# Three reorderings in a Mixture-of-Experts and Mamba kernel: copies of B ahead of evacuations on ScalarE, the last two state sums side by side on TensorE, and the fourth B multiply with the SiLU burst one tile on

## The chip, the cores and the metric

The kernel runs on one core of a Trainium2 chip. The metric is the device time of one execution in microseconds (µs). Before the change it is 6058.42 µs, the median of three runs (6050.98 to 6075.53).

## What is computed

Input x is (8, 96, 64, 64) in float32: 8 images of 4096 tokens with 96 channels. Two layers follow one another.

```python
# layer 0: mixture of 4 experts (hidden 192), the two best by router, added to x
logits = tokens @ router_w.T + router_b
gates  = softmax over the two best logits, 0 for the others
for ei in range(4):
    hid = gelu(tokens @ fc1_w[ei].T + fc1_b[ei])
    out = out + gates[..., ei:ei+1] * (hid @ fc2_w[ei].T + fc2_b[ei])
x = x + scale * out

# layer 1: layer norm over channels, a Mamba block forward and on the reversed sequence
xr, z = split(x_norm @ W_in)                  # 192 inner channels each
xr = silu(causal_conv4(xr) + conv_b)
dt = softplus(xr @ W_xproj[:, :6] @ W_dt + b_dt);  B, C = (xr @ W_xproj)[:, 6:]   # 16 states
h  = exp(dt * A) * h + (dt * xr) * B          # the scan over 4096 tokens
y  = sum over states of h * C + xr * D
out = (y * silu(z)) @ W_out
x  = (out_forward + out_reversed) * 0.5 + x
```

## The kernel before, in words

**Tiles.** The state has 192 channels times 16 states, 3072 rows, which make `NT` = 24 tiles of 128 partitions. A sequence is cut into 8 chunks of 512 tokens (`CH`). One *body* treats one chunk in one direction: 24 scans of 128x512. An image has 16 bodies, 8 forward (numbers 0 to 7) and then 8 reverse (8 to 15), and there are 8 images, so 128 bodies. Bodies are written in pairs, an even one (`odd` = 0) and an odd one (`odd` = 1), inside loops over images and pairs (`bodies`). In the text, scan i is the scan of tile i of a body.

**Batches.** Four tiles make a batch, so six batches (`NB`) to a body, numbered s = 0 to 5. The product dt\*x\*B of batches 0 and 1 is made by GpSimd (L1240, 128x2048), that of batches 2 to 5 by VectorE (L1147, 128x2048): these four are "the first to fourth B multiply" here, with `h` = 0 to 3. VectorE reads for them a copy of B that ScalarE puts into the PSUM bank `p_b` (`copy_b`, L927). There is one such bank, so copy h waits for multiply h-1. A multiply also waits for the sum of the batch that used its slot of X before (`summed_before`).

**The round of a tile.** ScalarE computes exp(dt\*A) into one of three PSUM banks (`exp_dA`, L939, two tiles ahead of the scan; exponential i waits for scan i-3). VectorE scans (L1163). When a batch of four is scanned, GpSimd saves the carries (L1248) and multiplies by C (L1250, 128x2048), and TensorE adds the states of that batch into the bank `p_y` (`sum_states`, L708). Sum 1 closes the low channels of y, sum 5 the high channels. After sum 5 the bank is emptied: in a forward body ScalarE evacuates it (`evacuate`, L944) to be stored; in a reverse body VectorE gates it (`gate_y`, L1168) with SiLU(z), and TensorE then makes the output (`finish`, L717 to L719), which ScalarE copies out (`copy_out`, L879). The work on sum 5 of a body lies in the first tiles of the next.

**Around the scans** each pair of bodies also carries the layers of later chunks. In the even body TensorE first sums and multiplies experts into the piece's output (`residual` L650, `expert_out` L656, `expert_bias` L660), ScalarE copies it (`copy_x2`, L868), then comes the layer norm (`ln_mean` L665, `ln_centred` L874 and L875, `ln_var` L669, `ln_rstd` L884 and L887). Each body has three hidden tiles of the experts (L640), with one GELU burst on ScalarE (a table load, three activations and a table load back, L861 and L852), gating rows on TensorE (L647) and three gate instructions on VectorE (L1127). TensorE projects the window for the convolution (L677). Near the end of a body ScalarE has the SiLU burst: a table load and two activations for xr (`silu_x`, L894), in most reverse bodies two for z (`silu_z`, L899), and a load back. TensorE then projects dt, B and C from xr (`project_dt`, L692 and L693), and at the start of the next body ScalarE and VectorE turn that into softplus(dt) (L909, L911, L915, L1135).

**What sets the order.** Nothing is scheduled. Every engine has its own stream written out by hand, in program order, with semaphore waits between engines. On ScalarE and VectorE the steps beside the scans hang on the tile number `i`, in the order of the `if` lines; on TensorE they are a plain list. All DMAs are on SyncE's queue.

The lines that hang on a tile number on ScalarE:

```python
if i == 5 and before == 0:
    evacuate(n - 1, 0, ...)
if i == 5:
    copy_b(n, 0, par)
...
if i == 8:
    if before == 1:
        copy_out(u)
    copy_b(n, 1, par)
```

`before` is 0 where the body before this one ran forward, 1 where it ran in reverse.

## Time and profile before

| what | value |
|---|---|
| median of the runs | 6058.42 µs |
| time of the profiled execution | 6065.3 µs |
| its span, first to last instruction | 6063.5 µs |
| mean granted clock of TensorE | 0.855 of full speed |
| VectorE busy | 5276.6 µs (87%), 4474 instructions |
| GpSimd busy | 5156.9 µs (85%), 2127 |
| TensorE busy | 4967.7 µs (82%), 14273 matmuls |
| ScalarE busy | 4307.0 µs (71%), 6471 |
| DMA | 159 GB/s over the span |

A row of a timeline gives the start from the beginning of the span, the duration, engine, line, operation, what it writes and reads, how many instructions are merged in it, and in brackets how long the engine was idle before it and which instruction released it. The first 190 µs are setup and routing, up to about 380 µs the first image's experts; then the 128 bodies follow until the end. A float32 matmul of this kernel shows as two records.

### The profile page before, as it was taken

The page shows a single profiled execution, that of the slowest core. Times are in us where ns is not written, and L with a number is a line of the kernel's source. Part 1 is how long each engine was busy: PE and PEld are TensorE (multiplying, and loading weights), DVE is VectorE, ACT ScalarE, POOL GpSimd, SP SyncE. Part 2 cuts the span into 40 slices and gives each one's busy share as a digit, 9 for nine tenths or more (in the row PEclk, how much of TensorE's full clock was granted, in tenths as well). Part 3 has the DMA queues.
Part 4 walks back from the last instruction along what each step waited for, and adds up shares of the span by engine and source line. Part 5 has one row for each costly group of instructions (what it writes and reads, how often), then busy time and mean ns, then how long its engine had stood idle before and what let it go on. Part 6 is the DMA issues. An engine that isn't in the chain of part 4 may idle for free.

```text
span 6063.5 us, 68824 instructions
## 1 busy us (share of the span) xinstructions
PE 4967.7 (82%) x14273; PEld 1536.1 (25%) x14273; DVE 5276.6 (87%) x4474; ACT 4307.0 (71%) x6471; POOL 5156.9 (85%) x2127
## 2 busy tenths in 40 slices
PE   7777888878888888888888778887888888888787
PEld 7222222222222222222222222222222222222222
DVE  1239989998999989999899999999899998999998
ACT  0447777777777777777777777777677777777776
POOL 0039989998899998999898998989899998999898
PEclk9878789888888888887898789878888888988898
DMA  3046767676676767676776767666676767766776
GB/s 94 22 98 163 168 164 175 160 174 157 166 173 156 176 155 175 166 171 160 169 173 159 171 160 173 166 163 169 159 175 163 171 161 171 170 165 165 170 172 149
DMA packets 428356, 964.98 MB, mean 159 GB/s; under 512 B 58080, under 2 KB 58329, under 8 KB 394984
## 3 DMA queue, kind: packets, MB, share of 16 engines
q1 hardware_dynamic: 428008, 961.31, 65.6%
q14 instruction: 247, 2.02, 0.1%
q8 instruction: 101, 1.65, 0.1%
HBM read 776.98 MB, written 184.11 MB: 159 GB/s over the span
## 4 chain that ended last, share of the span: by engine, by line
issue 25%; PE 25%; DVE 14%; DMA 10%; POOL 9%; ACT 7%; SPq 2%; DVEq 1%; ACTq 0%; POOLq 0%
DVE X L1163 11%; PE ps L677 8%; POOL X L1250 4%; DMA bc_d<-bc 3%; PE ps L708 3%; POOL X L1240 3%; DMA lo_d<-bc 3%; DMA lo<-lo_d 2%; PE ps L699 2%; PE ps L702 2%; PE ps L656 2%; ACT ps L939 1%; DVE X L1147 1%; PE ps L717 1%; DMA y_d<-yf 1%
## 5 line engine op out<-in xcount | busy, mean ns | idle before, releaser
L1250 POOL TENSOR_TENSOR X<-X,cR 128x2048 f32<-128x2048 f32 x768 | 3479.1, 4530 | 62.0
L1163 DVE TENSOR_TENSOR_SCAN X<-ps,carry,X 128x512 f32<-128x512 f32 x2688 | 3261.6, 1266 | 87.9 <-ACT ps L939 71.3
L939 ACT ACTIVATE ps<-hi,amat 128x512 f32<-128x512 f32 x2048 | 1377.1, 684 | 829.3 <-DVE X L1163 826.1
L1147 DVE TENSOR_TENSOR X<-hi,ps 128x2048 f32<-128x2048 f32 x512 | 1164.6, 2275 | 244.6 <-PE ps L708 133.7
L1240 POOL TENSOR_TENSOR X<-lo,bR 128x2048 f32<-128x2048 f32 x258 | 1168.5, 4529 | 21.8 <-DMA lo<-lo_d 21.8
L708 PE MATMUL ps<-X,red 128*32 128x512 f32 x6144 | 922.9, 676 | 305.6 <-POOL X L1250 304.5
L677 PE MATMUL ps<-win,w_u 97*128 97x512 f32 (+1 forms) x2080 | 1112.7, 684 | 5.9 <-DMA win<-xn_d 4.8
L939 ACT ACTIVATE ps<-lo,amat 128x512 f32<-128x512 f32 x1026 | 688.8, 679 | 163.1 <-DVE X L1163 120.7
L692 PE MATMUL ps<-xr,wd 128*96 128x512 f32 (+1 forms) x520 | 381.6, 826 | 280.4 <-ACT xr L894 227.3
L640 PE MATMUL ps<-xp,w 96*128 96x512 f32 x864 | 524.2, 738 | 54.8 <-DMA xp<-in_x 51.2
L677 PEld LDWEIGHTS ps<-win,w_u 97*128 97x128 f32 (+1 forms) x2080 | 369.7, 188 | 669.5 <-issue 634.5
L1248 POOL COPY carry<-X 128x4 f32<-128x4 f32 x768 | 144.5, 188 | 417.6 <-DVE X L1163 413.3
L1163 DVE TENSOR_TENSOR_SCAN X<-ps,X 128x512 f32<-128x512 f32 x384 | 444.8, 1206 | 30.9 <-POOL X L1240 19.5
L1127 DVE TENSOR_TENSOR hid<-ps,hid 128x512 f32<-128x512 f32 x432 | 289.8, 673 | 176.1 <-PE ps L647 174.9
L656 PE MATMUL ps<-hid,w 128*96 128x512 f32 x852 | 423.1, 617 | 0.0
L699 PE MATMUL ps<-xr,dg 64*128 64x512 f32 (+1 forms) x512 | 348.0, 766 | 74.2 <-DVE yr L1168 47.0
L708 PEld LDWEIGHTS ps<-X,red 128*32 128x32 f32 x6144 | 125.9, 112 | 985.0 <-POOL X L1250 573.8
L1213 POOL TENSOR_TENSOR xnp<-xc,sq 96x512 f32<-96x512 f32 x71 | 90.3, 1271 | 331.7 <-ACT sq L887 331.7
L693 PE MATMUL ps<-xr,wd 65*96 65x512 f32 (+1 forms) x520 | 353.0, 768 | 0.0
L852 ACT ACT_TABLE_LOAD x265 | 340.0, 1283 | 4.7
L927 ACT ACTIVATE ps<-bR 128x512 f32<-128x512 f32 x512 | 299.2, 584 | 0.0
L861 ACT ACTIVATE hid<-ps,b 128x512 f32<-128x512 f32 x432 | 271.2, 686 | 39.3 <-PE ps L640 37.2
(111 smaller groups left out, 4352.1 us busy)
## 6 DMA issues: line engine op xcount, KB each, us to landing
hi<-hi_d SPq DMA_DIRECT2D x516, 512.0 KB, 8.2
bR<-bc_d SPq DMA_DIRECT2D x516, 256.0 KB, 4.6
lo<-lo_d SPq DMA_DIRECT2D x516, 256.0 KB, 4.5
cR<-bc_d SPq DMA_DIRECT2D x516, 256.0 KB, 7.1
hi_d<-S SPq DMA_DIRECT2D x258, 256.0 KB, 8.0
y_d<-yf SPq DMA_DIRECT2D x128, 256.0 KB, 8.8
yb<-y_d SPq DMA_DIRECT2D x128, 256.0 KB, 7.4
win<-xn_d SPq DMA_DIRECT2D x130, 196.3 KB
```

The costliest lines, as they stand in the source:

```text
L640: ready(u, f"H{m}", mm(begin(u, f"H{m}")[:, :], w1[:, P * m:P * m + P], xp[:, :], start=True, stop=True))
L656: mm(p_w[u.at["Y2"][0]][0:C, :], w2[:, m, :], hid[:, m, :], start=False, stop=False)
L677: last = mm(out[0:m, :], w_u[:, t, a:a + m], win[:, par, at:at + CH], start=(t == 0), stop=(t == TAPS - 1))
L692: mm(out[0:m, :], w_d[0][:, a:a + m], xr[0][:, par, :], start=True, stop=False)
L693: ready(u, name, mm(out[0:m, :], w_d[1][:, a:a + m], xr[1][:, par, :], start=False, stop=True))
L699: mm(p_y[:, :], diag[low][:, :], xr[low][0:(P, DR)[low], par, :], start=True, stop=False, skip_group_check=True)
L708: last = mm(p_y[GRP * j:GRP * j + GRP, :], red[:, :], X[:, slot(par, s), j, :], start=False, stop=(s in (LOW - 1, NB - 1)), skip_group_che ...
L939: A_(p_a[i % RING][:, :], dt, ACT.Exp, scale=amat[:, column(i):column(i) + 1]).then_inc(s_exp, 1)
L1147: V.tensor_tensor(X[:, slot(par, s), :, :], hi[:, par, HIGH:2 * HIGH, :], p_b[:, :].unsqueeze(1).to_broadcast([P, BATCH, CH]), ALU.mult).t ...
L1163: V.tensor_tensor_scan(h, a, h, 0.0 if head else carry[:, i:i + 1], ALU.mult, ALU.add).then_inc(s_scan, 1)
L1240: G.tensor_tensor(batch(par, s), lo[:, LOW:2 * LOW, :].unsqueeze(1).to_broadcast([P, 2, 2, CH]), quads(bR, par, s), ALU.mult).then_inc(s_b ...
L1250: G.tensor_tensor(batch(par, s), batch(par, s), quads(cR, par, s), ALU.mult).then_inc(s_hc, 1)
```

## The change

On ScalarE the first copy of B moves from tile 5 (behind the evacuation of a forward y) to tile 4, and the second copy, at tile 8, moves ahead of the copy of the output. On TensorE, in even bodies, the sums 4 and 5 of the body before stand next to one another, and expert multiplies 3 and 4, which stood between them, follow. On ScalarE the SiLU burst moves from tile 19 to tile 20, and on VectorE the fourth B multiply moves from before scan 19 to before scan 20.

```diff
@@ -778,11 +778,9 @@
                         expert_out(m, u, None)
                     if before is not None:
                         sum_states(n - 1, NB - 2, nxt)
-                    expert_out(3, u, None)
-                    expert_out(4, u, None)
-                    if before is not None:
                         sum_states(n - 1, NB - 1, nxt)
-                    expert_out(5, u, None)
+                    for m in range(3, HT):
+                        expert_out(m, u, None)
                     expert_bias(u)
                 y_begin(1, n, f, par)
                 if not odd:
@@ -984,18 +982,18 @@
                         softplus_start(0, u, n + 1)
                     if i == 3:
                         softplus_log(0, n + 1)
+                    if i == 4:
+                        copy_b(n, 0, par)
                     if i == 5 and before == 0:
                         evacuate(n - 1, 0, img * NCH + (NCH - 1 if rev else q * 2 + odd - 1))
-                    if i == 5:
-                        copy_b(n, 0, par)
                     if i == 6 and not odd:
                         copy_x2(u, pc - 1)
                     if i == 7 and not odd:
                         ln_centred(u, pc - 1)
                     if i == 8:
+                        copy_b(n, 1, par)
                         if before == 1:
                             copy_out(u)
-                        copy_b(n, 1, par)
                     if i == 9 and not odd:
                         copy_gates(u)
                     if i == 10 and not odd:
@@ -1008,7 +1006,7 @@
                         evacuate(n, 1, img * NCH + q * 2 + odd)
                     if i == 16:
                         copy_b(n, 3, par)
-                    if i == 19:
+                    if i == 20:
                         silu_x(u, par)
                         if nrev:
                             silu_z(u, nxt)
@@ -1192,8 +1190,8 @@
                         gate_y(n, True, par)
                     if i in (14, 15, 16):
                         gate_hidden((3 if odd else 0) + i - 14, u)
-                    if i in (7, 11, 15, 19):
-                        times_b(n, i // 4 - 1, par)
+                    if i in (7, 11, 15, 20):
+                        times_b(n, (7, 11, 15, 20).index(i), par)
                     scan(n, i, rev, par, head)
```

How this moves instructions, at three places. All lines behind L778 are two lower after the change (L939 becomes L937, L927 becomes L925, and so on).

ScalarE at the start of a forward even body: exponentials into ps, the evacuation (yf<-ps) and the copy of B (ps<-bR). Before:

```order
L939 ACTIVATE ps<-lo,amat 128x512
L942 ISA
L943 ISA
L944 ACTIVATE yf<-ps 128x512
L925 ISA
L926 ISA
L927 ACTIVATE ps<-bR 128x512
```

After:

```order
L925 ACTIVATE ps<-bR 128x512
L934 REGISTER_ALU
L937 ACTIVATE ps<-lo,amat 128x512
L940 ISA
L941 ISA
L942 ACTIVATE yf<-ps 128x512
```

The copy of B stood behind the evacuation with its waits; now it stands an exponential ahead of it.

ScalarE in a reverse body, around the copy of the output (xf<-ps). Before:

```order
L845 REGISTER_ALU
L879 ACTIVATE xf<-ps 96x512
L926 REGISTER_ALU
L927 ACTIVATE ps<-bR 128x512
L936 REGISTER_ALU
```

After:

```order
L924 REGISTER_ALU
L925 ACTIVATE ps<-bR 128x512
L843 REGISTER_ALU
L877 ACTIVATE xf<-ps 96x512
L934 REGISTER_ALU
```

The two have changed places; L845 (now L843) is the wait for TensorE's output.

TensorE at the start of an even body: L708 is a state sum of four matmuls, L656 an expert multiply, L660 the expert bias. The difference:

```order
 L708 MATMUL ps<-X,red 32x512 x4
-L656 MATMUL ps<-hid,w 96x512 x2
-L706 REGISTER_ALU
-L708 MATMUL ps<-X,red 32x512 x4
-L656 MATMUL ps<-hid,w 96x512
+L706 REGISTER_ALU
+L708 MATMUL ps<-X,red 32x512 x4
+L656 MATMUL ps<-hid,w 96x512 x3
 L660 MATMUL ps<-gT,b2s 96x512 x3
```

Sum 5 is now directly behind sum 4, and the three remaining expert multiplies are behind both.

## Rows read from the trace of the kernel before

**Rows 1.** Busy time by window: core, PE, PEld, DVE, ACT, POOL, clock, DMA share, GB/s

```profile
4117.00:4200.10 83.10, 63.57 (x193) 18.40 (x186) 80.22 (x67) 64.98 (x99) 79.05 (x34) 0.86 0.71 171
3057.60:3146.40 88.80, 75.82 (x225) 22.85 (x224) 82.88 (x71) 66.09 (x101) 80.34 (x34) 0.90 0.69 169
```

**Rows 2.** Waits of VectorE, forward bodies 1 to 7 of one image: total, times, longest

```profile
DVE X L1147 <- ACT ps L927: 9.8, 6, 2.5
DVE X L1147 <- PE ps L708: 5.2, 4, 1.4
DVE X L1163 <- issue: 3.0, 1, 3.0
DVE X L1163 <- ACT ps L939: 2.2, 5, 0.7
```

**Rows 3.** Waits of VectorE, seven reverse bodies of one image

```profile
DVE X L1163 <- ACT ps L939: 6.3, 6, 1.4
DVE yr L1168 <- PE ps L708: 4.5, 4, 1.3
DVE X L1147 <- ACT ps L927: 4.4, 4, 1.2
```

**Rows 4.** Timeline, forward odd body: sum 5, evacuation, copy of B, first B multiply

```profile
4161.61 1.94 PE L708 MATMUL ps<-X,red 128*32 128x512 f32 x8 [3.42 <-POOL X L1250]
...
4163.61 0.60 ACT L944 ACTIVATE yf<-ps 128x512 f32<-128x512 f32 x1 [2.80 <-PE ps L708]
...
4164.10 0.60 ACT L927 ACTIVATE ps<-bR 128x512 f32<-128x512 f32 x1
...
4164.82 2.29 DVE L1147 TENSOR_TENSOR X<-hi,ps 128x2048 f32<-128x2048 f32 x1 [2.53 <-ACT ps L927]
```

**Rows 5.** Timeline, from SiLU through the next forward even body

```profile
4188.16 1.28 ACT L894 ACT_TABLE_LOAD   x1
...
4190.84 2.02 PE L692 MATMUL ps<-xr,wd 128*96 128x512 f32 x2 [5.43 <-ACT xr L894]
...
4198.81 4.54 POOL L1250 TENSOR_TENSOR X<-X,cR 128x2048 f32<-128x2048 f32 x1
...
4201.47 1.07 PE L708 MATMUL ps<-X,red 128*32 128x512 f32 x8
...
4215.15 1.28 ACT L861 ACT_TABLE_LOAD   x1
...
4219.60 0.69 ACT L939 ACTIVATE ps<-hi,amat 128x512 f32<-128x512 f32 x1
```

**Rows 6.** Timeline of VectorE: two dependent setup instructions; nine scans in a row

```profile
160.11 1.23 DVE L1105 TENSOR_TENSOR X<-X 128x1024 f32<-128x1024 f32 x1 [1.12 <-ACT X L840]
161.37 1.22 DVE L1106 TENSOR_REDUCE X<-X 128x256 f32<-128x1024 f32 x1
...
4189.51 10.68 DVE L1163 TENSOR_TENSOR_SCAN X<-ps,carry,X 128x512 f32<-128x512 f32 x9
```

**Rows 7.** Timeline of a reverse pair, odd body and then even body

```profile
3017.81 0.68 DVE L1168 TENSOR_TENSOR yr<-ps,sz 128x512 f32<-128x512 f32 x1
...
3034.60 1.28 DVE L1163 TENSOR_TENSOR_SCAN X<-ps,carry,X 128x512 f32<-128x512 f32 x1
...
3044.71 1.28 ACT L894 ACT_TABLE_LOAD   x1
...
3050.55 7.16 DVE L1163 TENSOR_TENSOR_SCAN X<-ps,carry,X 128x512 f32<-128x512 f32 x6 [0.85 <-ACT ps L939]
...
3069.87 0.60 ACT L879 ACTIVATE xf<-ps 96x512 f32<-96x512 f32 x1 [0.84 <-PE ps L719]
...
3078.97 0.69 ACT L939 ACTIVATE ps<-hi,amat 128x512 f32<-128x512 f32 x1
...
3093.74 1.09 PE L692 MATMUL ps<-xr,wd 128*96 128x512 f32 x2 [0.76 <-ACT sz L899]
```

**Rows 8.** Timeline of VectorE, first reverse body of an image, fourth B multiply

```profile
4325.64 2.29 DVE L1147 TENSOR_TENSOR X<-hi,ps 128x2048 f32<-128x2048 f32 x1 [8.11 <-PE ps L708]
```

## The prediction

> **What bounds the kernel now.** I read four views in this order: busy time by window, the waits of VectorE, the timeline around each wait, and the chain that sets each releaser. Times are µs. One trip of the loop is a body: 24 scans on VectorE, one sixth of the state tiles at a time through GpSimd, and there are 128 of them in pairs (even, odd). A forward pair takes 83.1 and holds 80.2 of VectorE work and 79.1 of GpSimd work; a reverse pair takes 88.8 and holds 82.9 and 80.3 [rows 1]. So neither engine is the bound by itself. VectorE is nearest to it, and what can be won is its waits. In one image's forward stretch of 303 µs they are 9.8 for a copy of B, 5.2 for a sum of TensorE, 3.0 in one piece that no engine released, 2.2 for an exponential [rows 2]. In the reverse stretch of 309 µs they are 6.3 for exponentials, 4.5 for the sum ahead of a gating, 4.4 for a copy of B [rows 3].
>
> Where the copy of B is late, in a forward odd body: TensorE ends the last sum, having begun at 4161.61 after 3.42 of waiting for GpSimd; ScalarE, which stood for 2.80 behind that sum, evacuates at 4163.61 and only then copies B at 4164.10; VectorE starts the first B multiply at 4164.82, 2.53 late [rows 4]. The copy itself needs nothing that is late. It only stands behind the evacuation.
>
> A second chain runs beside this, and it decides how much of the gain stays. From the table load of the SiLU burst (4188.16) TensorE projects dt (4190.84), sums, multiplies the experts and the mean of the layer norm, and ScalarE gets through the layer norm to the table load of GELU (4215.15) and to the exponential that scan 14 needs (4219.60 + 0.69) [rows 5]. That is 32.1 from load to exponential, with TensorE busy all the way to the mean.
>
> **The change part by part.** No instruction is added or taken out, so busy time stays. No DMA moves on a queue.
>
> *First copy of B, one tile sooner and ahead of the evacuation.* ScalarE's copy (pitch 0.5) lies beside 2 to 3 µs in which it waits anyway [rows 4]. The first B multiply no longer waits. What is late next is exponential 8, now behind the evacuation: it ends 0.6 + 0.7 after the evacuation starts, 4164.9, while VectorE, 2.53 earlier, would want scan 8 at 4162.3 + 2.2 + 1.2 = 4165.7. That leaves 0.8 of cover. If GpSimd were over 0.8 later against VectorE, the wait would come back there. So the 9.8 of [rows 2] go.
>
> *Second copy of B ahead of the copy of the output.* Reverse bodies only. In the odd body it takes away 1.1 of waiting (all of the 4.4 of [rows 3]). In the even body ScalarE waits 0.84 for the output [rows 7], so a copy of 0.53 now fits inside that wait, and all behind it comes 0.53 sooner.
>
> *Fourth B multiply one tile on.* It used to stand before scan 19, now before scan 20, which reads it. Its wait for the third sum (5.2 in four times, the longest 1.4 [rows 2]) shrinks by one scan, 1.18: nine scans in a row take 10.68 [rows 6]. The cost is that scan 20 follows directly the multiply that it waits for. In the setup, instructions that wait for the one in front start 1.26 after it where it takes 1.23 [rows 6], 0.03 behind its end; scans start 0.09 before the end of the one in front (1.27 long, pitch 1.18). The price is bounded by 0 and 0.12 per body; I take 0.1, since the setup rows are the same situation. The Trainium skill (VectorE: DVE Perf Modes, section The DRAIN you can't avoid) says that a semaphore after each VectorE instruction costs nothing extra; by that the price would be 0 and the sum some 6 µs lower. Here the measured rows decide.
>
> *SiLU burst one tile on.* It now starts behind exponential 22, thus behind scan 19 where it was behind scan 18. As the multiply also moved, scans 20 to 22 and the multiply cover it as scans 19 to 21 and the multiply did, so the wait of 0.85 in a reverse odd body (3050.55, 5.84 after the load at 3044.71) [rows 7] only moves to scan 23. But the second chain starts 1.18 later against the scans. How much work does VectorE have between the end of scan 19 and scan 14 of the next body? 18 scans 21.2, three B multiplies 6.6, two dt instructions 1.2, one gate 0.6: 29.6 to 29.8. The chain takes 0.83 (from scan to load) + 32.1 = 32.9. So in a forward even body like this one VectorE must wait **3.1**, before scan 14 or sooner. Counted from scan 18, before the change, it was 31.0 of work against 32.9. The chain is shorter where the projection runs at full clock: its four matmuls (two records each) are at most 0.93 faster each, by 2.02 in [rows 5] against 1.09 in [rows 7], 3.7 in all, and then nothing waits. Bounds 0 and 3.1; I take 2.75, near the slow end, since TensorE waited 5.43 ahead of the slow one and will wait longer.
>
> *Last two sums side by side.* In even bodies the last sum comes two expert multiplies (1.9) sooner. It must be ready: GpSimd ends it at 4198.81 + 4.54 = 4203.35, the sum before it ended at 4201.47 + 1.07 = 4202.5 [rows 5]. With SiLU 1.18 later the sum before ends at 4203.7, so TensorE does not wait and the expert work behind it comes no later than the chain above says. The gain goes to the evacuation (forward), which the moved copy of B has already made harmless, and to the first gating of the even reverse body (up to 1.3 late in [rows 3]).
>
> *Forward sum, per image.* Waits now 9.8 + 5.2 + 2.2 = 17.2, the 3.0 left alone. After: three even bodies with 2.75, 8.2; seven times 0.1, 0.7; 0.5 for what is left of the sums' waits. 9.4, so **−7.8 per image, −62 for eight**.
>
> *Reverse sum, per pair.* The bound is a ring. (a) Scan 19 of the odd body to scan 14 of the even one: 0.83 + (3078.97 + 0.69 − 3044.71 = 34.95) − 0.53 = 35.2. (b) Scan 14 to the end of scan 19: six scans, two gates, one multiply, 10.6. (c) From there to scan 14 of the odd body: 0.83 + 5.84 to scan 23, 9.4 of VectorE work to the gating, and from the gating (3017.81) through TensorE's output and GELU to scan 14 16.8 − 0.53 [rows 7]: 32.4. (d) 10.6 again. Together 88.8, what it is today. The 1.1 and 1.3 of [rows 3] that the moved copy and sum give back are spent on the later SiLU. **0 for the reverse half.**
>
> *At the turn* (first reverse body) VectorE waits 8.11 for a sum behind a load of y [rows 8], in front of the fourth multiply. One scan now runs before that wait, and SiLU waits there for TensorE and not for a scan: 1.18 − 0.1, eight times, **−9**.
>
> Sum: −62 − 9 = −71. The profiled execution took 6065.3 (span 6063.5, 1.8 around it), so 5994; the median of the runs shown is 6.9 lower, 6058.4, which gives **5987**.
>
> **The rivals.** *A, the second chain does not bind.* If TensorE projects at full clock in most bodies (L692 takes 1.09 at 3093.74 in [rows 7], 2.02 in [rows 5]) and the layer norm fits, only 1.2 per image of the 17.2 remain: −128 − 9, 5921. For it: reverse bodies do show the fast form. Against: in forward bodies TensorE waited 5.43 before it, and will wait longer.
>
> *B, the wait moves on.* VectorE arrives earlier at everything, and GpSimd, with 79.1 of 83.1 busy, lets the evacuation or the third sum be late again. If the forward stretch keeps 14 to 17 of its 17.2, the result is about 6030 to 6055, within 0.5% of now. For it: the 0.8 of cover is thin. Against: GpSimd is not slower than 81 per pair.
>
> *C, slower.* One mechanism: the projection of dt starts later after SiLU, in every body. In reverse ring (a) and (c) nothing is given back, so both 1.18 count: 28 pairs by 2.4 − 0.5, +53. TensorE's wait in front also grows, and the even reverse body's projection falls from the 1.09 of [rows 7] to the 2.02 of [rows 5] per matmul, up to 3.7; GpSimd's last product covers part of it, I count 0.8, +22. In forward bodies the chain then leaves 2 per image, −16, and the turn −9: +50, 6108. It decides where the wait before scan 14 in a reverse pair rises by over 2 per pair with the first gating no earlier. For the clock part the trace speaks: after a wait of 0.76 the matmul took 1.09 (2.4 GHz), after 5.43 it took 2.02 (1.2 GHz). The Trainium skill (TensorE: Matmul & The Clock Gate, Part 1) says that the throttled state is the default and activity releases it; by that rule, the trace agrees. Against C: the gating wait of 1.3 and the copy wait of 1.1 are real and go.
>
> *D, side by side does nothing or harms.* If GpSimd's last product comes after the sum before it, TensorE stands idle where it used to do two expert multiplies. By 4203.35 against 4202.5 that is 0.8, in 24 even forward bodies: 19 of the 71 lost, 6006.
>
> **How the numbers follow.** Forecast 45%, A 15%, B 20%, C 10%, D 10%. The forecast's own bounds (1.5 to 3.1 in the even body, 0 to 3 per image left of the sums' waits, ±0.7 per reverse pair from the clock) are 5950 to 6025. The range reaches to A below and over B above, **5920 to 6065**; C is left out. A difference under 0.5% (30 µs) cannot be told from none: 6028 and 6089 are the borders. Faster by over that: forecast, A, D, less 0.02 for their edges, 0.68. Within: B and those edges, 0.22. Slower: C, 0.10.
>
> **What would show it.** Waits of VectorE for a copy of B near zero; scan 14 in forward even bodies and the scans before it waiting 1.5 to 3.1 in all; a forward pair near 83.8; a reverse pair at 88.8 ± 0.5, with the wait before the first gating down and the one before scan 14 up to about 2.8 in the even body; scan 20 starting 2.3 after its multiply. The prediction is wrong if forward even bodies wait under 0.5 there (then A), or if the reverse pair moves by over 1.

## The result, and the profile after

The changed kernel takes 6084.23 µs (median of 16 runs, 6075.02 to 6099.53) against 6057.14 of the kernel before (median of 16, 6048.09 to 6075.53). The ratio is **1.0045, 95% interval 1.0035 to 1.0055**: slower by 27, at the edge of what was called no change. The forecast was 5987, 97 less, and the result lies outside the range.

| | before | after |
|---|---|---|
| profiled execution / its span | 6065.3 / 6063.5 | 6075.0 / 6073.2 |
| mean granted clock | 0.855 | 0.858 |
| VectorE busy | 5276.6 | 5289.9 |
| TensorE busy | 4967.7 | 4910.8 |

The two profiled executions differ by 9.7 where the medians differ by 27, since the one of before is above its median and the one of after the lowest of its runs. So what follows in the traces accounts for 10 of the 27, and two profiles can each be off by some 10.

Windows of a forward and a reverse pair after the change, to be read against [rows 1] (core, window, busy time of PE, PEld, DVE, ACT, POOL, clock, DMA share, GB/s):

```profile
4115.60:4199.50 83.90, 67.84 (x195) 19.61 (x194) 80.62 (x67) 64.99 (x99) 80.31 (x34) 0.82 0.70 170
3764.20:3853.10 88.90, 73.97 (x225) 23.00 (x224) 83.17 (x72) 66.26 (x101) 80.82 (x34) 0.92 0.70 169
```

The forecast had a forward pair near 83.8 and a reverse pair at 88.8; these two pairs meet it. Over the 24 odd-even pairs of bodies 9 to 14, reverse pairs went from 88.9 to 89.5 on the mean. In the even body that the forecast was worked from, the waits of the second chain are 1.27 before scan 10, 0.86 before a gate instruction and 0.72 before scan 14, 2.85, where 3.1 was worked out for it and 2.75 taken. Waits of VectorE in forward bodies 1 to 7 of the same image as [rows 2]:

```profile
DVE X L1161 <- ACT ps L937: 7.3, 8, 1.5
DVE X L1161 <- issue: 4.4, 1, 4.4
DVE hid L1125 <- PE ps L647: 3.6, 5, 1.8
DVE X L1161 <- DVE X L1145: 1.5, 7, 0.2
DVE X L1145 <- PE ps L708: 0.8, 3, 0.3
```

The copy of B (9.8) is gone and the third sum fell from 5.2 to 0.8. But 17.6 of waits stand where the four rows of [rows 2] add up to 20.2: exponentials, gating rows of the experts (L647) and the stall without a releaser took most of it back. In seven reverse bodies, against [rows 3]:

```profile
DVE X L1161 <- ACT ps L937: 10.5, 12, 1.5
DVE yr L1166 <- PE ps L708: 6.4, 6, 1.6
DVE X L1161 <- DVE X L1145: 1.5, 7, 0.2
```

The 4.4 for a copy of B is gone, and exponentials (6.3 to 10.5) and gatings (4.5 to 6.4) took it up.

**Where the time is, by region.** From the timelines of VectorE, each body is counted from its own tile 4 to tile 4 of the next, and summed over eight images (the reverse part without the last tiles of the program). The third column is the best version found below, the change without its SiLU part:

| region | before | after | without SiLU part |
|---|---|---|---|
| forward bodies 0 to 7 | 2763.6 | 2756.7 (−7) | 2737.8 (−26) |
| turn, body 8 | 401.8 | 418.6 (+17) | 406.2 (+4) |
| reverse bodies 9 to 15 | 2435.1 | 2437.0 (+2) | 2395.6 (−40) |

The forecast, in the same regions, was −62, −9 and 0. By bodies the picture is sharper. In the forward half the first two bodies of the images became 14 longer and bodies 2 to 7 became 21 shorter, of which odd bodies gave 48 and even ones took back 27. In the reverse half odd bodies 9 to 15 gave 35 and even bodies took 37.

The 14 hold one stall. Before scan 0 of body 2, in the second to the seventh image, VectorE and ScalarE stand together, for the most part without a releaser. After the change:

```profile
4027.46 3.63 DVE L1161 TENSOR_TENSOR_SCAN X<-ps,carry,X 128x512 f32<-128x512 f32 x3 [4.40 <-issue]
4027.49 0.69 ACT L937 ACTIVATE ps<-lo,amat 128x512 f32<-128x512 f32 x1 [4.88 <-issue]
```

It is the place where the loop over images goes back to its start. In the stretch from 30 before to 6 behind it there are 13 packets of the two instruction queues, and around the start of any other body at most 5. VectorE's waits there add up to 19.3 before the change and 32.1 after it. No run tested what sets them.

**A forward odd body, before and after.** These are the same body of the same image (3367 to 3411). VectorE before the change:

```profile
3387.40 0.67 DVE L1127 TENSOR_TENSOR hid<-ps,hid 128x512 f32<-128x512 f32 x1
3393.14 0.67 DVE L1127 TENSOR_TENSOR hid<-ps,hid 128x512 f32<-128x512 f32 x1
3397.93 2.29 DVE L1147 TENSOR_TENSOR X<-hi,ps 128x2048 f32<-128x2048 f32 x1 [0.58 <-PE ps L708]
3400.14 2.45 DVE L1163 TENSOR_TENSOR_SCAN X<-ps,carry,X 128x512 f32<-128x512 f32 x2
```

and after it:

```profile
3384.98 0.69 DVE L1125 TENSOR_TENSOR hid<-ps,hid 128x512 f32<-128x512 f32 x1 [0.84 <-PE ps L647]
3392.44 0.69 DVE L1125 TENSOR_TENSOR hid<-ps,hid 128x512 f32<-128x512 f32 x1 [1.61 <-PE ps L647]
3398.10 2.29 DVE L1145 TENSOR_TENSOR X<-hi,ps 128x2048 f32<-128x2048 f32 x1 [0.26 <-PE ps L708]
3400.60 2.46 DVE L1161 TENSOR_TENSOR_SCAN X<-ps,carry,X 128x512 f32<-128x512 f32 x2 [0.21 <-DVE X L1145]
```

VectorE comes to the first gate instruction 3.3 sooner (2.55 of it by the copy of B, the rest from the body before), and then waits 0.84, 1.61 and 0.26 for TensorE. The body took 43.3 before and takes 43.3 now. TensorE in the same body, before the change:

```profile
3385.32 1.03 PE L647 MATMUL ps<-gT,gsel 12*128 12x512 bf16 x2
3386.28 5.63 PE L677 MATMUL ps<-win,w_u 97*128 97x512 f32 x8
3391.85 0.39 PE L647 MATMUL ps<-gT,gsel 12*128 12x512 bf16 x1
```

and after it:

```profile
3370.55 1.49 PE L708 MATMUL ps<-X,red 128*32 128x512 f32 x8 [2.58 <-POOL X L1248]
3376.51 1.94 PE L708 MATMUL ps<-X,red 128*32 128x512 f32 x8 [1.70 <-POOL X L1248]
3384.34 1.03 PE L647 MATMUL ps<-gT,gsel 12*128 12x512 bf16 x2
3385.30 6.79 PE L677 MATMUL ps<-win,w_u 97*128 97x512 f32 x8
3392.02 0.39 PE L647 MATMUL ps<-gT,gsel 12*128 12x512 bf16 x1
```

The third gating row stands behind the projection of the window, and that takes 6.79 where it took 5.63 before, and 3.70 in a stretch at full clock. The granted clock of the two stretches (window, length, busy time of PE, PEld, DVE, ACT, POOL, clock, DMA share, GB/s), before and then after:

```profile
3386.30:3391.90 5.60, 5.60 (x10) 2.27 (x9) 5.60 (x6) 4.18 (x7) 5.60 (x2) 0.65 0.99 255
3385.30:3392.10 6.80, 6.80 (x10) 2.61 (x9) 5.53 (x5) 3.63 (x7) 6.72 (x4) 0.54 0.93 249
```

So TensorE runs almost the whole projection at the lower level (1.2 GHz) after the change, and most of it before. Ahead of it TensorE waits 2.58 and 1.70 for GpSimd; before the change these two waits were 3.67 and 1.23, so their length does not explain the slower projection. TensorE begins the first two gating rows 1.0 sooner than before the change and the third one 0.2 later, although VectorE comes 3.3 sooner. VectorE had 0.9 of cover at that gating row before (3391.85 + 0.39 against 3393.14), which no row in the prediction showed.

**A reverse even body after the change.** VectorE, then ScalarE:

```profile
3776.68 1.28 DVE L1161 TENSOR_TENSOR_SCAN X<-ps,carry,X 128x512 f32<-128x512 f32 x1 [0.62 <-ACT ps L937]
3783.32 0.69 DVE L1166 TENSOR_TENSOR yr<-ps,sz 128x512 f32<-128x512 f32 x1 [0.81 <-PE ps L708]
3786.89 1.28 DVE L1161 TENSOR_TENSOR_SCAN X<-ps,carry,X 128x512 f32<-128x512 f32 x1 [1.11 <-ACT ps L937]
```

```profile
3772.12 0.59 ACT L866 ACTIVATE x2p<-ps 96x512 f32<-96x512 f32 x1 [3.47 <-PE ps L660]
3774.99 0.59 ACT L872 ACTIVATE sq<-ps 96x512 f32<-96x512 f32 x1 [1.70 <-PE ps L665]
3777.49 0.59 ACT L877 ACTIVATE xf<-ps 96x512 f32<-96x512 f32 x1 [0.32 <-PE ps L719]
```

Exponential 10 stands on ScalarE behind three copies that wait for the second chain (experts 3.47, mean of the layer norm 1.70, output 0.32), so VectorE now waits 0.62 before scan 10, where it did not wait before (14.9 in all even reverse bodies, 0 before the change). That is the second chain of the prediction, coming through at a tile earlier than scan 14.

### The profile page after: what moved, and what is told of

Its sections match the earlier page's. It is cut to its first block, busy times and chain, and to the rows that moved or that the text cites. A ratio compares the mean times of both kernels' runs of the same rounds, so it can differ in the third digit from the quotient of the medians.

```text
span 6073.2 us, 68824 instructions
## 1 busy us (share of the span) xinstructions
PE 4910.8 (81%) x14273; PEld 1555.8 (26%) x14273; DVE 5289.9 (87%) x4474; ACT 4302.1 (71%) x6471; POOL 5156.5 (85%) x2127
## 3 DMA queue, kind: packets, MB, share of 16 engines
q14 instruction: 247, 2.02, 0.1%
## 4 chain that ended last, share of the span: by engine, by line
DVE 24%; PE 23%; issue 21%; ACT 14%; DMA 5%; POOL 3%; SPq 1%; DVEq 1%; ACTq 1%; POOLq 0%
DVE X L1161 15%; DVE X L1145 6%; PE ps L656 4%; PE ps L677 4%; PE ps L708 3%; ACT ps L937 3%; DMA bc_d<-bc 2%; POOL X L1248 2%; PE ps L692 2%; DVE hid L1125 2%; ACT L892 2%; PE ps L693 2%; ACT L850 2%; ACT L859 1%; ACT xr L892 1%
## 5 line engine op out<-in xcount | busy, mean ns | idle before, releaser
L937 ACT ACTIVATE ps<-hi,amat 128x512 f32<-128x512 f32 x2048 | 1386.2, 684 | 879.9 <-DVE X L1161 876.0
L677 PE MATMUL ps<-win,w_u 97*128 97x512 f32 (+1 forms) x2080 | 1082.2, 669 | 5.9 <-DMA win<-xn_d 4.9
L708 PE MATMUL ps<-X,red 128*32 128x512 f32 x6144 | 859.7, 642 | 190.8 <-POOL X L1248 190.5
L937 ACT ACTIVATE ps<-lo,amat 128x512 f32<-128x512 f32 x1026 | 689.8, 676 | 112.6 <-DVE X L1161 48.6
L692 PE MATMUL ps<-xr,wd 128*96 128x512 f32 (+1 forms) x520 | 457.9, 979 | 353.6 <-ACT xr L892 300.6
L640 PE MATMUL ps<-xp,w 96*128 96x512 f32 x864 | 508.0, 720 | 65.3 <-DMA xp<-in_x 63.5
L1125 DVE TENSOR_TENSOR hid<-ps,hid 128x512 f32<-128x512 f32 x432 | 287.3, 667 | 198.1 <-PE ps L647 197.0
L656 PE MATMUL ps<-hid,w 128*96 128x512 f32 x852 | 404.4, 607 | 0.0
L699 PE MATMUL ps<-xr,dg 64*128 64x512 f32 (+1 forms) x512 | 319.7, 708 | 103.5 <-DVE yr L1166 66.8
L693 PE MATMUL ps<-xr,wd 65*96 65x512 f32 (+1 forms) x520 | 399.5, 862 | 0.0
L708 PEld LDWEIGHTS ps<-X,red 128*32 128x32 f32 x6144 | 130.5, 110 | 848.8 <-POOL X L1248 427.4
L682 PE MATMUL ps<-win,w_g 97*128 97x512 f32 x256 | 165.6, 733 | 187.6 <-ACT xr L892 187.0
L925 ACT ACTIVATE ps<-bR 128x512 f32<-128x512 f32 x512 | 297.9, 582 | 0.0
```

Source lines behind the costliest of these rows:

```text
L640: ready(u, f"H{m}", mm(begin(u, f"H{m}")[:, :], w1[:, P * m:P * m + P], xp[:, :], start=True, stop=True))
L656: mm(p_w[u.at["Y2"][0]][0:C, :], w2[:, m, :], hid[:, m, :], start=False, stop=False)
L677: last = mm(out[0:m, :], w_u[:, t, a:a + m], win[:, par, at:at + CH], start=(t == 0), stop=(t == TAPS - 1))
L692: mm(out[0:m, :], w_d[0][:, a:a + m], xr[0][:, par, :], start=True, stop=False)
L693: ready(u, name, mm(out[0:m, :], w_d[1][:, a:a + m], xr[1][:, par, :], start=False, stop=True))
L708: last = mm(p_y[GRP * j:GRP * j + GRP, :], red[:, :], X[:, slot(par, s), j, :], start=False, stop=(s in (LOW - 1, NB - 1)), skip_group_che ...
```

## The experiments

Fourteen kernels were run, each beside runs of the kernel before on the same chip. The parts are: the first and the second copy of B, the sums side by side, the multiply, SiLU.

### Single parts

**Both copies of B alone.**

```diff
+                    if i == 4:
+                        copy_b(n, 0, par)
...
-                    if i == 5:
-                        copy_b(n, 0, par)
...
                     if i == 8:
+                        copy_b(n, 1, par)
                         if before == 1:
                             copy_out(u)
-                        copy_b(n, 1, par)
```

> Only the two copies of B are moved. Theory L (the loss of the whole change comes from the late SiLU burst and from the multiply directly in front of its scan): the copies alone gain, 25 to 60 us (ratio 0.990 to 0.996), VectorE's waits for a copy of B fall from 107.8 us to under 10. Rival R (whatever wait is taken from VectorE comes back at once behind another engine): 0 to -10 us, with waits for exponentials up by what the copies gave.

Measured 6094.06, ratio 1.0059 (1.0043 to 1.0075): **slower by 36**, though every wait for a copy of B is gone. Neither theory allowed a loss. By region it is −10 in the forward half, +2 at the turn and +36 in the reverse half. In odd forward bodies, 52.8 of waits for the copy go, and 35.6 come back at gating rows and 6.8 at the third sum; in reverse bodies the first gating of even bodies waits 56.0 instead of 28.3. The mean granted clock was 0.834 to 0.846 in the six runs, against 0.850 to 0.856 before, and the time at the lower level, behind the first 380 µs, 1908 instead of 1700. In a reverse pair of 92.1 TensorE projects the window and dt so:

```profile
1665.69 7.08 PE L677 MATMUL ps<-win,w_u 97*128 97x512 f32 x8
1682.61 1.09 PE L692 MATMUL ps<-xr,wd 128*96 128x512 f32 x2 [0.76 <-ACT sz L899]
1710.28 3.70 PE L677 MATMUL ps<-win,w_u 97*128 97x512 f32 x8
1727.26 2.02 PE L692 MATMUL ps<-xr,wd 128*96 128x512 f32 x2 [0.76 <-ACT sz L899]
```

Both L692 rows follow a wait of 0.76 and yet take 1.09 and 2.02 (granted clock 1.00 and 0.50). So the length of the wait just in front does not tell the clock, as the prediction had argued from two rows. The saved waits came back as waits for gating rows (174.9 in the whole program to 216.8), for the third sum (133.7 to 152.2), for exponentials (81.7 to 128.2) and for gatings of y (75.2 to 109.9). Why reverse bodies lose more than the copy gave was not settled.

**Sums side by side alone.**

```diff
                         sum_states(n - 1, NB - 2, nxt)
+                        sum_states(n - 1, NB - 1, nxt)
-                    expert_out(3, u, None)
-                    expert_out(4, u, None)
...
```

> Only the last two sums are side by side. Theory L: no change, -8 to +8 us. Rival S (TensorE now stands idle before the last sum, where it did two expert multiplies, and everything behind comes later): +15 to +40 us, with TensorE's wait for GpSimd's last product in even bodies up by 0.8 us each.

Measured 6074.55, 1.0031 (1.0019 to 1.0042): slower by 16, as rival S had it. S's mark is in the trace too: in even bodies TensorE waits 61.7 for GpSimd's last product where it waited 7.9, 0.84 per body. The gatings of y wait far less (75.2 to 21.4), the copies of B too (107.8 to 72.4), but the B multiplies wait for sums 187.2 instead of 133.7.

**The multiply alone.**

```diff
-                    if i in (7, 11, 15, 19):
+                    if i in (7, 11, 15, 20):
```

> Only the fourth B multiply is moved to before scan 20, SiLU stays. In the changed kernel scan 20 starts 2.50 us after its multiply, where before the next scan started 2.21 after it: 0.29 x 128 = 37 us of cost. Theory L: this cost less what the shorter waits for the third sum give, so -20 to +20 us. Rival R: the full +37 us.

Measured 6036.41, 0.9966 (0.9955 to 0.9977): faster by 22, just past the good end of theory L. Waits for the third sum fall from 133.7 to 77.3, and the row of a scan that waits for its multiply appears with 22.3.

**SiLU alone**, the multiply left before scan 19.

```diff
-                    if i == 19:
+                    if i == 20:
                         silu_x(u, par)
```

> Only the SiLU burst is moved to tile 20; the multiply stays before scan 19. Theory L: the projection of dt and all that hangs on it start 1.18 us later; slower by 30 to 100 us (ratio 1.005 to 1.017), in reverse bodies above all. Rival S: no loss from SiLU, -5 to +10 us.

Measured 6475.07, 1.069 (1.0669 to 1.0711): slower by 417, four times the upper end of theory L. The burst stands behind exponential 22, which waits for scan 19, and scan 19 here stands behind the multiply, so the burst starts a multiply and a scan later (3.4), and only scans 20 to 22 cover it, without the multiply. VectorE there:

```profile
3785.51 2.29 DVE L1147 TENSOR_TENSOR X<-hi,ps 128x2048 f32<-128x2048 f32 x1 [1.43 <-PE ps L708]
3787.72 4.80 DVE L1163 TENSOR_TENSOR_SCAN X<-ps,carry,X 128x512 f32<-128x512 f32 x4
3796.52 1.28 DVE L1163 TENSOR_TENSOR_SCAN X<-ps,carry,X 128x512 f32<-128x512 f32 x1 [4.00 <-ACT ps L939]
```

Waits for exponentials are 445.1 in the program where they were 81.7, and that is most of the 417. The multiply and the burst belong together, as the prediction had said.

### Parts together

**Copies and sums.** The edits of the first two.

> The copies and the sums without multiply and SiLU. If the parts add up: +36 +16, 6105 to 6115. If the sums side by side only shift the same wait that the copies open (theory R), the two together cost what the copies alone do, 6090 to 6098.

Measured 6042.92, 0.9966 (0.9953 to 0.9979): faster by 17, which neither expectation allowed. Alone the two cost 36 and 16; together they win. Effects of single parts here do not add up: +36 + 16 against −17. The first gating of even reverse bodies, which waited 56.0 with the copies alone, waits 4.9 here.

**Copies, sums and multiply**: the whole change without SiLU.

> The whole change without the SiLU part (burst back at tile 19, multiply stays before scan 20). Theory L (the later SiLU burst costs most of the loss): 6040 to 6055, 30 us or more below the changed kernel. Theory K (copies and sums lose by themselves, because the gap that TensorE gets elsewhere lets its clock fall; the SiLU move, covered by the moved multiply, costs nothing): the three parts add up, +36 +16 -22 = +30, so 6080 to 6095, like the changed kernel.

Measured **6002.86, 0.9909 (0.9887 to 0.9931)**: faster by 57 than before and by 81 than the change. That is better than theory L had it, and theory K fell. It is the best version that was found.

**Multiply and SiLU.**

> Only the fourth multiply and the SiLU burst move (both one tile on); copies and sums stay. Theory L: slower than the multiply alone (6036) by 30 us or more, 6065 to 6085. Theory K: SiLU adds under 10, so 6030 to 6046.

Measured 6115.89, 1.0095 (1.0077 to 1.0113). Against the multiply alone (6036) that is +80, against +81 with the copies and sums in place. The price of the later SiLU is the same with and without the rest, above the 6065 to 6085 of theory L. It is spread differently, though. From the profiled executions, against the kernel before (a difference of two single profiles in one region can be off by some 10):

| version | forward | turn | reverse |
|---|---|---|---|
| copies | −10 | +2 | +36 |
| sums | −12 | +8 | +14 |
| multiply | −14 | −7 | −7 |
| copies, sums | −11 | +18 | −29 |
| copies, sums, multiply | −26 | +4 | −40 |
| multiply, SiLU | +24 | 0 | +19 |
| the change | −7 | +17 | +2 |

The later SiLU costs 38, 7 and 26 in the three regions behind the multiply alone, and 19, 12 and 41 behind the other three parts.

**Two other tiles for SiLU**, 18 and 17, with copies, sums and the multiply at 20.

```diff
-                    if i == 20:
+                    if i == 18:
                         silu_x(u, par)
```

> The change with the SiLU burst at tile 18 on ScalarE instead of 20 (copies of B, sums side by side and the multiply at 20 kept); beside the version with it at 19 (6003) and the change itself with it at 20 (6084). Theory P, the SiLU burst anchors a chain (projection of dt, sums, experts, layer norm, GELU, exponentials) that binds in most bodies, and each tile of 1.18 us costs about 0.63 us per body: with the slope unbroken 6003 - 80 = 5923; expected 5930 to 5975, because the waits left before scan 14 and the gatings are already small in the version at 19. Theory Q, the price of 80 us was a collision that only tile 20 has (the burst directly in front of the last exponentials, and scan 23 waiting for it), and nothing is to be won by going sooner: 6003 within 15. Theory R, sooner is also worse, because the convolution of the window is not ready by tile 18, or scan 21 waits for its exponential: above 6020.

> As the version with the SiLU burst at tile 18, with the burst at 17. Theory P: the gain per tile falls as the chain stops binding and other waits (GpSimd is busy 79 to 80 of a pair of 83 to 89) take over: 5900 to 5970, at most 25 below tile 18. Theory Q: 6003 within 15. Theory R: the burst now waits for the convolution's last matmuls, exponential 19 or 20 is late, above 6020.

| SiLU at tile | time, ratio (95%) | forward | turn | reverse |
|---|---|---|---|---|
| 20 | 6084.23, 1.0045 (1.0035 to 1.0055) | 2756.7 | 418.6 | 2437.0 |
| 19 | 6002.86, 0.9909 (0.9887 to 0.9931) | 2737.8 | 406.2 | 2395.6 |
| 18 | 6020.56, 0.9939 (0.9925 to 0.9952) | 2735.0 | 399.1 | 2415.5 |
| 17 | 6084.88, 1.0040 (1.0026 to 1.0053) | 2772.7 | 387.3 | 2463.4 |

The theory that each tile sooner wins (P) fell: 18 is 18 slower than 19, and 17 is 82 slower. Both times lie where theory R had them. Only the turn goes by P, 48.4, 49.9, 50.8 and 52.3 per image from tile 17 to 20, 1.3 per tile where a scan is 1.18. At 17 the price is plain, in VectorE's rows from the fourth multiply on and in ScalarE's table load of the burst:

```profile
3714.64 2.29 DVE L1145 TENSOR_TENSOR X<-hi,ps 128x2048 f32<-128x2048 f32 x1
3719.51 9.51 DVE L1161 TENSOR_TENSOR_SCAN X<-ps,carry,X 128x512 f32<-128x512 f32 x8 [2.58 <-ACT ps L937]
3713.68 1.28 ACT L892 ACT_TABLE_LOAD   x1 [1.89 <-PE ps L677]
```

The burst there comes before exponential 20. Scans 17 to 19 and the multiply cover it, as three scans and the multiply do at the other tiles; what is new is that ScalarE stands 1.89 in front of the table load until TensorE has projected the window, and all of the burst and exponential 20 come later by that. These waits for SiLU at tile 19, 18 and 17:

```profile
ACT L892 <- PE ps L677: 47.1, 9, 13.4
ACT L892 <- PE ps L677: 114.4, 72, 13.3
ACT L892 <- PE ps L677: 175.9, 93, 13.5
```

So theory R's reason, that the window is not ready, is what the traces show: 9 waits at 19, 7 of them at the turn, became 93 at 17. VectorE's waits for exponentials are 343.8 in the program at 17, against 124.7 at 19. At 18 they are 184.9; before scan 21 there is a wait in nearly every reverse body and before scan 10 in most even ones, while gatings fall from 76.4 to 26.8. Why reverse bodies lose 20 at 18 was not settled; only 17 of the 114.4 lie there.

**Without the second copy.** As the best version, but the second copy of B stays behind the copy of the output.

> The three parts without SiLU (6003), but the second copy of B left behind the copy of the output, as before the change. It acts in reverse bodies alone. If the second copy is worth what the waits of VectorE for it showed (4.4 us per image before the change), the time is 6003 + 20 to 35, 6023 to 6038. If the reverse bodies are bound by the chain through the copy of the output and the layer norm, putting the copy of B ahead costs what it gains: 6003 within 10. If it harms by delaying the output: below 5993. Alone with the first copy, without the other parts, the two copies cost 36 us; this run tells whether the second has a share in that.

Measured 6039.28, 0.9966 (0.9952 to 0.9979): the second copy is worth 36, just past the upper end of what was expected. The waits of VectorE for it were 36.8 in the reverse bodies of the kernel before, so with the first copy, the sums and the multiply there it is worth what its row says. What it is worth without them was not run.

### Does the forward gain hang on the place of the gate instructions?

The gate instructions of the experts (L1125) were moved on VectorE, in the whole change, in the best version, and for the third instruction alone.

```diff
-                    if i in (14, 15, 16):
-                        gate_hidden((3 if odd else 0) + i - 14, u)
+                    if i in (15, 16, 18):
+                        gate_hidden((3 if odd else 0) + (15, 16, 18).index(i), u)
```

> The whole change, and on VectorE the three gate instructions of the experts (L1125) go from ahead of scans 14, 15, 16 to ahead of scans 15, 16, 18. After the change VectorE waits 32 us in forward bodies ahead of scan 14 and some 15 ahead of scan 16 for gating rows that TensorE makes before and behind its half-clock projection of the window (L677, 6.79 for eight matmuls at 3385.30). Theory G, those waits are what the forward gain turned into and only their place is at fault: they fall from 47 to under 10 and the time goes 25 to 40 us down, 6045 to 6060. Theory H, the forward bodies are bound by a ring (GpSimd's products, sums, TensorE at half clock, SiLU), and VectorE then waits the same elsewhere (fourth B multiply for the third sum, scan 14, scan 10 of the next body): 6084 within 12.

> The three parts without SiLU (6003), with the gate instructions ahead of scans 15, 16, 18. Its waits for gating rows are 29 and 23 us ahead of scans 16 and 14 in forward bodies (60 in all without the first image's experts). Theory G: 6003 - 40 = 5963, between 5950 and 5975. Theory H: 6003 within 12, the wait ahead of the fourth B multiply up from 0.25 per odd body to 1 to 2.

> As the one before, but only the third gate instruction moves, from ahead of scan 16 to ahead of scan 17: the 29 us ahead of scan 16 shrink by one scan each (25 times up to 1.18). Theory G: 6003 - 20 to 28, 5975 to 5983. Theory H: 6003 within 10.

Measured 6107.89, 1.0084 (1.0070 to 1.0097), so +24 to the change; 6051.25, 0.9984 (0.9973 to 0.9996), +48 to the best version; and with the third alone 6012.34, 0.9919 (0.9907 to 0.9932), +9, which the two intervals do not tell from none. Theory G fell, and H was right in kind, though moving all three costs more than H allowed. In the best version a forward odd body has these waits on VectorE (3331 to 3375):

```profile
3349.63 0.69 DVE L1125 TENSOR_TENSOR hid<-ps,hid 128x512 f32<-128x512 f32 x1 [0.83 <-PE ps L647]
3357.42 0.69 DVE L1125 TENSOR_TENSOR hid<-ps,hid 128x512 f32<-128x512 f32 x1 [1.94 <-PE ps L647]
3363.08 2.29 DVE L1145 TENSOR_TENSOR X<-hi,ps 128x2048 f32<-128x2048 f32 x1 [0.25 <-PE ps L708]
```

and one with the gate instructions late has one wait in their place (3364 to 3407):

```profile
3395.74 2.29 DVE L1145 TENSOR_TENSOR X<-hi,ps 128x2048 f32<-128x2048 f32 x1 [2.76 <-PE ps L708]
```

0.83 + 1.94 + 0.25 = 3.02 became 2.76. In even forward bodies, all eight images, the waits for exponential 14 went from 28.4 to 75.4 while those for gating rows went from 24.1 to 0. VectorE waits at least the same wherever the gate instructions stand, and a wait taken away at one meeting point is found again at the next. So what binds the forward bodies lies with the other engines; which of them was not singled out by a run.

**More work for TensorE.** To test whether the lower clock can be kept away, eight bf16 matmuls that add zero went ahead of the projection of dt, and eight between the last two sums of odd bodies, in the whole change.

> The changed kernel, and on TensorE eight small bf16 matmuls that add zero to the open y bank, in two places where TensorE waits: before the projection of dt in every body (behind the z projection) and between the last two sums in odd bodies. The output stays the same. Theory K: the time that TensorE spends at half clock (1670 us in the changed kernel) falls below 1200, and the kernel gets faster by 20 to 80 us (6005 to 6065). Theory L or R: the clock is not on the path, no change or a small loss from the added work, 6080 to 6110.

Measured 6213.68, 1.0243 (1.0221 to 1.0265), slower than any theory had it. The time at the lower clock, summed from the clock records behind the first 380 µs, did not fall (1810 against 1670 in the change). The added matmuls took 434 of TensorE's time, and the projection of dt began 4.6 behind the table load of its burst on the mean instead of 3.6. What the clock costs in this kernel stays open: in the 16 runs of the change those at 0.854 and 0.855 took 6090 to 6100 and those at 0.859 and 0.860 6077 to 6087, but the runs of the kernel before, at 0.850 to 0.856, show no such relation.

## Why the prediction was wrong, point by point

**The waits for copies of B: right in the main.** In all forward bodies they were 69.5 (forecast 78, from one image) and are zero; in reverse bodies 36.8, zero now. The waits are gone as forecast; that they would turn into time is what failed, as told below.

**Third sum in forward bodies: right.** 41.1 before, 5.6 after, −35.5 where the forecast had −38.

**The second chain in forward even bodies: right in size.** The forecast was 2.75 per body before scan 14 or sooner. Waits for exponentials 9 to 14 and gating rows are now 87 in 32 even bodies, 2.7 each: 16.5 before scan 10, 33.6 before scan 14, 33.5 at gate instructions, the rest before scans 9 and 13. The largest two of these terms were 16.4 and 17.9 before. The three together rose by 49, and the forecast for the rise was (8.2 − 2.2) × 8 = 48. But its cause is only half right: without the SiLU part they are 60 already, so about 25 of the 49 come with the other three parts, and 24 from the later burst.

**The reverse ring: the number right, in part by luck.** Forecast 0, measured +2. Without the later SiLU the reverse bodies gain 40, and the later SiLU takes 41: that what the copy and the sum give back is "spent on the later SiLU" is what the runs show, but 1.4 won and 1.5 spent per pair instead of 2.4 each. Two terms that were both too large cancel. And the prediction's signs for this half did not come: the wait before the first gating of even bodies was to go down and stayed (28.3 and 27.9), the one before scan 14 was to rise to 2.8 and fell (28.4 to 17.5 in 24 even bodies). The waits stand before scan 10 (0 to 14.9) and at the second gating (1.8 to 28.7) instead.

**The step that failed first: the rest of the forward sum**, "seven times 0.1, 0.7; 0.5 for what is left of the sums' waits". It said that nothing else would be late in forward bodies, and so booked each removed wait in full. Forecast for the forward half −62, measured −7. Of the gap of 55, the trace has:

- the dependent scan: it starts 2.50 after its multiply (3398.10, 3400.60) where a scan started 2.21 after it before (3397.93, 3400.14). That is 0.29, not 0.1, and lies outside the bound of 0.12 that the setup rows gave. It is 0.29 in 106 of the 128 bodies and 0.1 to 0.2 in the others. In the forward half it makes 16.8 instead of 5.6. The rows of the setup were another kind of instruction pair: their first one was no multiply of 128x2048 and their second no scan. The Trainium skill (VectorE: DVE Perf Modes, section The DRAIN you can't avoid) says that a semaphore after each instruction costs nothing extra; by the row above, waiting for the one of the instruction directly in front does cost here;
- odd bodies and the first tiles behind them: gating rows +7.2, the exponential that waits for the burst +9.1 (scan 22 before, scan 23 now), scan 3 of the next body +3.1;
- the stall without a releaser before scan 0 of body 2, 19.3 to 32.1. It was left alone in the forecast. Over the sixteen traces its total is 6.5 (SiLU at tile 17) to 32.1, and no run settled what sets it;
- 11 by which the copies and sums were smaller over eight images than in the one that was read.

These make 54 of the 55. The first and the last are sizes; the two in the middle are waits that the sum put at nothing. The run without the SiLU part shows the step by itself: in odd forward bodies the gating rows wait 35.6 there, 6.3 before the change, where VectorE comes sooner than TensorE is ready for it.

**The turn: wrong in sign.** Forecast −9, measured +17. The term itself, one scan ahead of the wait for the load of y, was right: the multiply alone gives −7, and its wait falls from 59.5 to 44.5. What failed is that it was the only term. The later SiLU adds 7 (to the multiply alone) or 12 (to the other three parts), and the copies and the sums, which the forecast had at nothing here, add 11 to 18 (18 by themselves). With these two the wait at the gating before scan 13 is 37.5 instead of 23.1. In the whole change the second chain shows before scans 9, 10 and 14 instead (0 before, 27.7 in eight images), and the load of y is waited for by TensorE, and its sum by VectorE:

```profile
5020.44 2.08 PE L702 MATMUL ps<-yb,ident 128*128 128x512 f32 x2 [6.54 <-DMA yb<-y_d]
5029.17 2.29 DVE L1145 TENSOR_TENSOR X<-hi,ps 128x2048 f32<-128x2048 f32 x1 [8.49 <-PE ps L708]
```

That the turn goes 1.3 per tile over four places of the burst shows that the burst has a share in its time. By what way is read from the chain of waits in this stretch, in which stores on SyncE's queue (lo_d<-bc, y_d<-yf) stand between the projected B and C and this load; that part, and how the copies and sums act here, was only read, not tested.

**The rivals.** The result lies between B (6030 to 6055) and C (6108). B's mechanism is the nearest to what the forward bodies show: without the stall that nothing releases, they keep 147 of their 173 of waits in eight images. B named the evacuation and the third sum as the places, and it is the gate instructions and scans 10, 14 and 23; it also had the turn at −9. C is refuted by its own mark: the waits before scan 14 in reverse bodies went from 28.4 to 23.9. Yet its core, that the later SiLU costs in the reverse ring too, is right, and its +53 there was 41. A is refuted: forward even bodies wait 2.7 each. D's 19 is near the 16 that the sums cost alone, and there its mark is in the trace (7.9 to 61.7). But with the copies in place the sums win 51 (6094 to 6043), and in the change itself TensorE waits 7.7 at that place, as before, so D is not what the change shows.

**What the sum hid.** Without SiLU, the forecast's own terms are −110 in forward bodies (−62 − 48), −67 in reverse pairs (28 by 1.1 + 1.3) and −9 at the turn, −186; the runs show −57 for all of it. The forecast's terms for SiLU are +48 and +67, +115; the runs show +81. So the gains were three times overrated, and the price by two fifths. The direction hung on the difference: the gains that are real, 57, are smaller than the price that is real, 81, and 57 − 81 leaves the 24 to 27 by which the change is slower.

## What to carry to other kernels

A step that opens a chain for another engine has its price in every type of body, and it can be had in one run by moving that step alone, one place each way: here one tile later cost 81 and one sooner 18. Before a removed wait is booked as gain, read the cover at each later place where the engine meets another one (here 0.9 at a gating row). Here, of the 52.8 that the copies alone took from odd forward bodies, 42.4 stood at the next two meeting points. Parts that each lose alone can win together, so a change of several parts is judged by leaving one out as well as by doing one alone.

## What the runs showed of the hardware

- A scan that waits for the 128x2048 multiply directly in front of it starts up to 0.29 later than one that doesn't; 0.21 of it is shown as a wait, the rest is lost overlap. In 128 bodies of the change this is 34, more than half of what the best version wins.
- The projection of the window takes 3.70 (granted clock 1.00) to 7.08 (0.52) for the same eight matmuls, and projections of dt 1.09 or 2.02 after an equal wait of 0.76. Eight bf16 matmuls of filler at two places did not lower the time at the lower clock level (1810 against 1670).
- Moving two copies of 0.6 on ScalarE changed the mean granted clock of TensorE from 0.855 to 0.839 in the profiled executions.
- Where the loop over images goes back to its start, VectorE waits 0.9 to 6.8, mostly with no releaser, in every version, and the instruction queues move 12 or 13 packets around it, against at most 5 around the start of any other body.
